# Fill of a two-layer attention and expert kernel: spread units one per step, a shorter run-ahead, and maxima transfers issued by ScalarE

## The reference

```python
x = x + _L0_xattn_ref(_layernorm(x, axis=-1), ctx_1024, ctx_1024, 16)
x = x + _L0_ffn_ref(_layernorm(x, axis=-1), L0_ffn_rms_w, ...)
x = x + _L1_xattn_ref(_layernorm(x, axis=-1), ctx_1024, ctx_1024, ...)
x = x + _L1_ffn_ref(_layernorm(x, axis=-1), L1_ffn_gate_w, ...)
```

## Time and profile before

| what | value |
|---|---|
| median of 3 runs | 1141.96 us (1137.48 to 1150.51) |
| the profiled execution | 1142.05 us |
| its span (first to last instruction) | 1140.2 us |
| TensorE busy (matmul) | 926.6 us, 81% |
| VectorE busy | 616.8 us, 54% |
| ScalarE busy | 545.9 us, 48% |
| GpSimd busy | 321.5 us, 28% |

### The profile page before, as it was taken

The page is one execution under the profiler, slowest core; times in us unless marked ns, Lnnn a source line. Parts: engine busy times, 40 slices in busy tenths (PEclk is TensorE's granted clock), DMA queues, the critical chain, the costliest instruction groups (busy, mean ns, idle before and its releaser), DMA issues. The chain is left out here.

```text
span 1140.2 us, 16688 instructions
## 1 busy us (share of the span) xinstructions
PE 926.6 (81%) x6470; PEld 618.8 (54%) x6470; DVE 616.8 (54%) x1007; ACT 545.9 (48%) x829; POOL 321.5 (28%) x307
## 2 busy tenths in 40 slices
PE   3665989899447999994859998999985429999994
PEld 2422334343347999992634334444434428999894
DVE  7585788793450111113575466678715545566553
ACT  4444677678302233322546566576761205554550
POOL 1387554000002222222124522110000344455322
PEclk9957899999658999997878999999996559999997
DMA  5026572600226999986011927060005214345516
GB/s 223 12 89 149 141 169 74 100 4 3 82 101 228 334 344 342 350 308 163 27 62 57 188 112 142 31 101 15 4 2 198 100 51 116 112 127 162 137 20 166
DMA packets 45153, 146.59 MB, mean 129 GB/s; under 512 B 7096, under 2 KB 24248, under 8 KB 34808
## 3 DMA queue, kind: packets, MB, share of 16 engines
q1 hardware_dynamic: 30800, 111.21, 32.5%
q0 software_dynamic: 14288, 34.48, 11.3%
HBM read 110.15 MB, written 34.47 MB: 127 GB/s over the span
## 5 line engine op out<-in xcount | busy, mean ns | idle before, releaser
L871 DVE TENSOR_REDUCE a_row_max<-ps_ring 128x2 f32<-128x1024 f32 x256 | 309.7, 1222 | 134.9 <-PE ps_ring L636 132.8
L804 ACT ACTIVATE a_probs<-ps_ring 128x1024 f32<-128x1024 f32 x256 | 260.9, 1023 | 111.7 <-PE ps_ring L653 110.1
L672 PE MATMUL ps_out<-a_probs,a_vaug 128*32 128x256 f32 x2048 | 166.9, 399 | 2.5 <-ACT a_out_sb L810 1.5
L636 PE MATMUL ps_ring<-a_ka,a_qa 52*128 52x512 f32 (+1 forms) x512 | 118.5, 465 | 37.2 <-DVE a_row_max L871 15.2
L653 PE MATMUL ps_ring<-a_qa,a_ka 56*128 56x512 f32 (+1 forms) x512 | 131.3, 510 | 4.5 <-DMA a_qa<-a_max_t 3.7
L1074 ACT ACTIVATE e_hid<-ps_ring,e_wts 128x128 f32<-128x128 f32 x184 | 52.2, 368 | 110.4 <-PE ps_ring L1134 80.8
L653 PEld LDWEIGHTS ps_ring<-a_qa,a_ka 56*128 56x128 f32 (+1 forms) x512 | 48.9, 187 | 98.5 <-issue 64.6
L1421 ACT ACTIVATE e_hr<-ps_ring 128x512 fp32r<-128x512 f32 x64 | 38.3, 598 | 117.6 <-PE ps_ring L1482 117.6
L1482 PE MATMUL ps_ring<-e_xt,e_wr 128*128 128x512 f32 x384 | 90.2, 394 | 2.7 <-DVE e_xt L1550 2.7
L1134 PEld LDWEIGHTS ps_ring<-e_xst,e_wts 128*128 128x128 f32 x736 | 87.7, 196 | 2.1 <-issue 1.0
L1134 PE MATMUL ps_ring<-e_xst,e_wts 128*128 128x128 f32 x736 | 88.0, 279 | 0.6 <-DVE e_xst L1231 0.6
(11 more groups left out here) (249 smaller groups left out, 1327.5 us busy)
## 6 DMA issues: line engine op xcount, KB each, us to landing
e_wts<-in_w SPq DMA_DIRECT2D x23, 1156.0 KB, 8.1
e_wts<-in_w SPq DMA_DIRECT2D x23, 1024.0 KB, 7.6
e_wf<-in_w SPq DMA_DIRECT2D x16, 1024.0 KB, 5.5
scratch_k_scr<-a_kst POOLq DMA_DIRECT2D x18, 512.0 KB, 4.6
scratch_q_scr<-a_qst POOLq DMA_DIRECT2D x36, 256.0 KB, 3.3
a_qa<-scratch_q_scr SPq DMA_DIRECT2D x24, 384.0 KB, 11.4
a_ka<-scratch_k_scr SPq DMA_DIRECT2D x24, 384.0 KB, 13.3
a_ctx_t<-in_ctx_t SPq DMA_DIRECT2D x8, 512.0 KB, 5.8
```

What stands on the lines that cost most here:

```text
L636: ins = pe.matmul(to[:, par], qa[rows, b % 2, g, p, qt * P:(qt + 1) * P], ka[rows, b % 2, g, p], start=True, stop=True)
L672: ins = pe.matmul(m.ps_out[VW * h:VW * (h + 1), cols], vaug[:, b % NV, kc, HG * g + h], probs[:, t % 3, h, cols], start=(kc == 0 and half ...
L804: nc.scalar.activation(probs[:, t % 3, 2 * half:2 * half + 2], unit("s", n), ACT.Exp, scale=HD ** -0.5).then_inc(exp_done, 1)
L871: dve.tensor_reduce(row_max[:, s % 3, qt, :, p], unit("m", n), AX.X, ALU.max).then_inc(mx_read, 1)
```

## The change

- Two numbers: `AHEAD` 7 for 8, and `SPREAD_AT` a table that puts the six units of groups 1 to 3 one by one at the *end* of steps -7, -6, -5, -3, -2 and -1. Group 0's are still spread ahead of the first maxima.
- The table of jobs is placed anew: the maxima transposes of slot s at step 4s - 3 (4s - 4 before), two steps ahead of the slot's scores; query, key and value pieces a few steps later than before; loads of batch 1 at steps 6 and 7.
- Statistics: batch 1 alone at step -3; those of batches 2 and 3 in steps 0 to 6, two tiles a step, then the chain of small ops.
- The zero fills go from VectorE to GpSimd; ScalarE's `last_rows` copies come behind its first jobs, and `marks_set` counts twice in layer 0.
- GpSimd rotates the keys of batch 1 ahead of the loop, before the units are spread; keys 2 are rotated at step 2 (-1 before), values at 16b - 11.
- `load_max` is issued by ScalarE, right behind its copy of the maxima, and no more by SP.

```diff
-AHEAD = 8
-SPREAD_AT = (-8, -7, -6, -5)
+AHEAD = 7
+SPREAD_AT = {-7: ("k", 1), -6: ("q", 1), -5: ("k", 2), -3: ("q", 2), -2: ("k", 3), -1: ("q", 3)}
...
     for s in range(SLOTS):
-        put(("m", s), 4 * s - 4)
+        put(("m", s), 4 * s - 3)
...
@@ attention, GpSimd @@
+                pool.memset(marks[:, 0:3 * H // 2 * MARK].bitcast(F32), 0.0).then_inc(marks_zero, 1)
+                if layer == 0:
+                    pool.memset(others[:, 0:H * P].bitcast(F32), 0.0).then_inc(marks_zero, 1)
...
                     if layer == 0:
-                        chain.link(rotate_keys(pool, chain, b))
+                        if b > 1:
+                            chain.link(rotate_keys(pool, chain, b))
...
                 values(0)
-                pool.wait_ge(spread, 2 * NG)
+                if layer == 0:
+                    chain.link(rotate_keys(pool, chain, 1))
+                    keys(1)
                 for par in range(2):
+                    pool.wait_ge(spread, 2 * NG)
...
-                            if t == max(16 * b - 33, -AHEAD):
+                            if b > 1 and t == 16 * b - 30:
                                 keys(b)
-                            if t == 16 * b - 13:
+                            if t == 16 * b - 11:
                                 values(b)
@@ attention, ScalarE: load_max moved here from SyncE @@
+                def load_max(s):
+
+                    b, g = s // NG, s % NG
+                    act.wait_ge(misc_free, index["m", s] + 1)
+                    if b >= 2:
+                        act.wait_ge(st_full, 8 * (s - 2 * NG + 1))
+                    for par in range(2):
+                        rows = slice(par * HALF_P + M_ROWS, par * HALF_P + S_ROWS)
+                        act.dma_start(qa[rows, b % 2, g].bitcast(F32),
+                                     max_t[MAX_ROWS * par:MAX_ROWS * (par + 1), s % 2].bitcast(F32).unsqueeze(1).to_broadcast([MAX_ROWS, PAIR, T])).then_inc(max_in[s % 2], 16)
...
                         nc.scalar.copy(max_t[:, s % 2], misc[0:2 * MAX_ROWS]).then_inc(misc_free, 1)
+                        load_max(s)
@@ attention, VectorE @@
                 for t in steps:
                     if t == TB - AHEAD:
-                        tile_stats(1, B)
+                        norms(range(TB, 2 * TB))
+                    if 0 <= t < 4:
+                        ins = tile_stats(range(2 * TB + 2 * t, 2 * TB + 2 * t + 2))
...
+                    if 4 <= t < 6:
+                        ins = tile_means(range(2 * TB + 4 * (t - 4), 2 * TB + 4 * (t - 3)))
...
+                    if t == 6:
+                        norm_scale(range(2 * TB, NT))
```

More of the change, by code:

```diff
@@ L144, in ring_schedule @@
     for t in range(-AHEAD, STEPS):
[L145 to L148, removed]
         for half in range(2):
+            if t == -AHEAD and half == 0:
+                put("k", 0)
+                put("q", 0)
             for kind, n in (("s", 2 * t + half), ("m", 2 * (t + AHEAD) + half)):
@@ L359, in load @@
                     g0, g1 = groups(part)
+                    if part == 1 and b >= 2:
+                        sp.wait_ge(mx_full, 8 * (NG * (b - 1) + g0) + 1)
                     for par in range(2):
@@ L738, in act_job, with spread_rows @@
                         nc.scalar.copy(att_t[:, c], misc[:]).then_inc(misc_free, 1)
+                def spread_rows(kind, g):
+                    dst, n_to = (ka, S_ROWS if layer == 0 else M_ROWS) if kind == "k" else (qa, M_ROWS)
+                    act.wait_ge(spread, 2 * g + (1 if kind == "k" else 2))
+                    for par in range(1 if g == 0 else 2):
+                        rows = slice(par * HALF_P, par * HALF_P + n_to)
+                        ins = nc.scalar.copy(dst[rows, 0, g], unit(kind, g)[rows])
+                    ins.then_inc(spread_act, 1)
                 def normed(i):
-                    act.wait_ge(stats_done, 1 if i < 2 else 2)
+                    act.wait_ge(stats_done, min(i // 2, 2) + 1)
                     if i >= 2:
@@ L780, in _ @@
                 if layer == 0:
+                    of = m.ident[:, 0:HALF_P].rearrange("p (a h i) -> p h a i", a=2, i=BIAS_ROWS)
+                    act.wait_ge(marks_zero, 2)
+                    for n in range(2):
+                        nc.scalar.copy(last_rows[:, n].rearrange("p h (a m) -> p h a m", a=2)[:, :, :, QK_ROWS:M_ROWS], of)
+                    for row in range(MAX_ROWS):
+                        ins = nc.scalar.copy(last_rows[:, 0].rearrange("p (g b) (a m) -> p g b a m", b=PAIR, a=2)[:, :, row % PAIR, :, M_ROWS + row],
+                                             m.ident[:, HALF_P:HALF_P + 1].unsqueeze(2).to_broadcast([P, NG, 2]))
+                    ins.then_inc(marks_set, 1)
                     act.wait_ge(turned, 1)
@@ L824, in added, with tile_stats @@
                     chain.link(ins)
[L826 to L829 removed]
+                def tile_stats(tiles):
                     for i in tiles:
```

85 lines of the change are left out of this document (36 added, 49 removed).

## The result

The changed kernel takes 1222.54 us (median of 4 runs, 1216.94 to 1230.37) against 1141.91 before: a ratio of 1.0701, 95% interval 1.0604 to 1.0798. It is 80 us slower, far outside the range of 1109 to 1165. The profiled execution took 1217.4 us, its span 1215.4, so the two profiles differ by 75.2 us. I account for those.

A forecast was written before the change was run, and what follows sets the result against it. TensorE was taken as the bound in mid attention, VectorE and ScalarE close. Layer 0: 12 + 5 − 17.6 = −0.6; layer 1: 12 + 2 − 11.7 = 2.3; with half the start's 1.5, 3.2 off 1142.05: about 1138.5, range 1109 to 1165.

The forecast's parts named there:

- Start of layer 0: Up to the first spread at 19.30: between 1.6 us sooner and 1.2 later, taken as no change.
- Keys of batch 1 ahead of the loop: Layer 0 start: GpSimd's key rotation contends with seven VectorE ops, q_ready 5 us late (0 to 7).
- The fill: Layer 0, first maxima to first scores: 29.8 us plus 2 for the clock, before 44.1; scores at 65.0.
- gain of 5 us in the first exps: Layer 0, first half steps of attention: five of them at the higher clock give 5 us.
- Layer 1's fill: Start of layer 1's attention: first exp 14 us sooner, less 2 for the clock, so 12.
- Load of batch 1: Layer 0, hole up to 114: data lands at 106.5, layer 0 12 us ahead, some 7 us of hole left.
- Statistics: Layer 1, steps 0 to 6: 13 chained small ops, some meeting GpSimd, cost 1.5 us.
- Two steps of lead "taken as enough": Maxima transfers: some 5 us for 16 KB to land, cost taken as 0, otherwise 1 to 2 us a slot.
- 5 us gained by leaving SyncE's queue: Layer 0, wait at 218.73: 3.67 us go, and an estimated 1.5 at the lower clock behind them.
- The price of ScalarE's issues: Each attention slot: two issues take 1.35 us of ScalarE's stream; 17.6 us in layer 0, 11.7 in layer 1.
- rival C: Behind each maxima job: stalls paid in full, TensorE's clock falls; 1176.5, or 1162.5 with half the clock's part; chance 0.21.
- Rivals A and B: A: ScalarE's issues take next to no time, 1109, chance 0.22. B: lock doesn't bite at the start, 1131.5, 0.12.

The follow-up runs named there:

- Half the hold: Kernel before, SyncE still issuing, with one extra 8x768 copy on ScalarE behind each slot's copy of the maxima: 1159.37 us, 1.0132.
- the full one: Kernel before, SyncE still issuing, with one extra 8x1536 copy on ScalarE behind each slot's copy of the maxima: 1194.25 us, 1.0414.
- experiment 5: Changed kernel with GpSimd's rotation of keys 1 held back until both query parts of the first tiles are ready: 1211.27 us, 1.0611.
- the issue move: Kernel before with only the two issues of each slot's maxima transfer moved from SyncE to ScalarE: 1220.98 us, 1.0717.

## Why the prediction was wrong

- **Start of layer 0: right.** "I take no change": the first spread stands at 19.71, 0.4 later. The scale chain did meet the fills (one op of 2.90 us at 6.19), and what was saved elsewhere made up for it.
- **Keys of batch 1 ahead of the loop: right.** I took 5 us of delay (0 to 7): q_ready came some 6.5 later, and the first maxima matmul stands at 35.32 for 28.18, so 7.1 later, the upper end of what I gave.
- **The fill: mechanism right, gain over-forecast in layer 0.** From the first maxima matmul to the first scores it is 37.4 us (72.69 − 35.32) where I had 29.8 + 2, and 44.1 before. The clock was 0.65 between 28 and 51 us, where I had assumed the higher level but for 2 us. In three other kernels with the same start the same stretch took 30.5, 31.8 and 33.3 us, the first two with the clock at 0.87 and 0.86 between 28 and 51, so the chain of the fill was sized rightly (last section). The gain of 5 us in the first exps fell away with the low clock, which was 0.74 from 73 to 86.
- **Layer 1's fill: right.** 12.1 us sooner, forecast 12.
- **Load of batch 1.** I had a hole of 7 us left of 12.45. In the changed kernel no wait for keys shows at all, since the attention came so late that the load was there. GpSimd's chain behind the spreads was right (27.0 us from the last evacuation at 74.83 to SyncE's first issue at 101.84, 29.5 forecast), but it began 10 us later than I had it.
- **Statistics: mis-sized.** I put 1.5 us on the 13 chained ops. In layer 0 they took 6.3 us, and the scores waited 4.91.
- **Two steps of lead "taken as enough", and 5 us gained by leaving SyncE's queue: a second step that failed.** Six late landings, 25.5 us, in place of the 5 us gained. I had taken the 3.67 us before as a matter of the queue. But the transfers land late behind a batch's loads from whichever queue they come, 21.4 us with SyncE's issues and the same steps: one issued by ScalarE at 227.21, 2 us behind the loads, released the scores at 241.28, with the DMA engines busy all the while:

```profile
233.00:241.00 8.00, 0.99 (x12) 0.42 (x4) 1.71 (x3) 0.51 (x1) 1.70 (x2) 0.71 1.02 169
```

- **The price of ScalarE's issues: the step that failed.** The wait was sized rightly: 1.33 to 1.36 us for two issues (1.35 forecast), waits of 34.0 us in all (29.3 forecast). What I left out of the sum, and gave to rival C at 0.21, is the clock behind the wait. The busy time of TensorE grew by 22.2 + 16.2 = 38 us in the two attentions, some 32 of it by the clock, with the late landings having their share in it. Half the hold costs 15 us, the full one 52. The evidence against C, a wait of 1.16 us that "did nothing that I can see", was one gap; in the same trace the one of 3.67 was followed by a low clock (1.03 and 1.08 us for the next weigh matmuls in place of 0.64), and 1.5 lies between.
- **Rival C** named the mechanism with 39 for the waits and 28 for the clock, and came to 1176.5 from a sum that still held the gains of the fill, the load and the transfers. In layer 0 none of these gains came: not the 12 of fill and load (step 9's scores start at 121.96, 119.33 before), not the 5 of the first exps, and the transfers' 5 turned into 22 more of waits (25.5 for 3.7). Rivals A and B are refuted by the 1.36 us of issue and by the VectorE rows of experiment 5.

The 77 us of the issue move then consist of some 52 for the hold (24 of them more waiting for ScalarE, 18.7 + 8.9 us in the two layers against 3.0 + 0.2 before, and most of the rest the clock) and some 25 that the hold alone doesn't give. The 25 is a difference of two medians; 12 of it show in the profiles, 8 as later landings and 4 as longer waits, and the rest stays open. (The terms of the prediction's sum give 1138.8 and not 1138.5, which changes nothing.)

The issues took 0.65 us each on ScalarE, and the exp behind them started when the second was over (195.93 + 1.36, and the exp at 197.40). The Trainium skill (Perfetto Trace Analysis, "DMA Instruction — HWDGE") says that the reported window of such an issue ends when the sequencer is free for the next instruction; the trace agrees.

## What to carry to other kernels

Put no DMA issue into the stream of an engine on whose every instruction the bound engine depends: here 1.36 us a slot on ScalarE cost 67 to 77 us, and two thirds of that came back with a mere copy in the place of the issues, half as waits and half as TensorE's lower clock behind them. Keep small transfers that someone waits for out from behind large loads, on whatever queue. Before a queue's waits are moved away, look what they pace: with the transfer between them the two halves of a load went out 12 us apart (139.53 and 151.68), without it 5. And place GpSimd's two-input work where VectorE has no ops that someone waits for: one such move brought the first exp 6 to 13 us forward, a second took a chain from 6.3 to 2.6 us, with no gain in the whole that can be told.

## What the runs showed that I had not expected

- Extra work made the kernel faster: four useless matmuls in each of 18 waits (1.06 us in the trace) took 21 us off the median. In layer 0, where 14 of them lie, the clock was 0.88 rather than 0.83.
- The cost of a hold is not proportional: 0.83 us a slot gave 15 us, 1.47 us gave 52. The clock fell behind some waits of 1.5 us and not behind others (283.20 and 299.17 above); what decides between these two wasn't tried.
- The same instructions up to the first exp ran at different clocks. Two of the spread matmuls in the changed kernel, and the same two in the one with SyncE's issues:

```profile
39.20 0.63 PE L591 MATMUL ps_ring<-a_kst,a_ka 128*128 128x512 f32 x1
49.27 0.63 PE L593 MATMUL ps_ring<-a_qa 128*128 128x512 f32 x1
```

```profile
39.06 0.40 PE L605 MATMUL ps_ring<-a_kst,a_ka 128*128 128x512 f32 x1
48.05 0.39 PE L607 MATMUL ps_ring<-a_qa 128*128 128x512 f32 x1
```

  Up to 38.7 us both kernels take 0.63 for such a matmul. The column of the granted clock shows 1.00 for the second from 28 us on, which its matmuls contradict, so I go by their lengths. The first exp stood at 76.3 or 72.2. In the kernel with four extra matmuls (none of them so early) and in that with ScalarE's issues and the loads apart it stood at 69.3 and 70.6. A forecast of such a fill can't be better than these 7 us.
